# Gated cross-attention and mixture of experts: spacing GpSimd's indirect transfers and reordering the seam between the two halves

## The reference

```
x   = x + tanh(g_xattn) * xattn(layernorm(x), ctx)     # x (16, 256, 128), ctx (16, 64, 128), 16 heads of 8
x   = x + tanh(g_ffn)   * moe(layernorm(x))
xattn: q, k, v = linear maps; softmax over 64 keys, masked, / sqrt(8); output map
moe:  logits = h @ router_w + router_b;  expert = argmax(logits)       # 8 experts
      u = h @ w1[expert] + b1[expert]        # 128 -> 1024, halves a and g
      y = (a * sigmoid(g)) @ w2[expert] + b2[expert]                   # 512 -> 128
```

## Time and profile before

| | |
|---|---|
| runs | 280.64, 278.85, 280.49 us, median 280.49 |
| profiled execution | 280.14 us, span of its instructions 278.0 us |
| busy: PE, DVE, ACT, POOL | 245.6, 209.0, 156.7, 158.5 us |
| granted TensorE clock, mean | 0.976 |
| first half, about | 0 to 144 us |
| expert stage, about | 146 to 268 us |

### The profile page before, as it was taken

The page is one execution under the profiler, slowest core; times in us unless marked ns, Lnnn a source line. Parts: engine busy times, 40 slices in busy tenths (PEclk is TensorE's granted clock), DMA queues, the critical chain, the costliest instruction groups (busy, mean ns, idle before and its releaser), DMA issues.

```text
span 278.0 us, 8458 instructions
## 1 busy us (share of the span) xinstructions
PE 245.6 (88%) x2411; PEld 184.2 (66%) x2411; DVE 209.0 (75%) x608; ACT 156.7 (56%) x436; POOL 158.5 (57%) x254
## 2 busy tenths in 40 slices
PE   3979999999999989989599899399979999999950
PEld 2554445555555555544248899299979999999940
DVE  6988998898989879879649489276757777776720
ACT  5487978777566566545086765256434444444410
POOL 6505426259677585384833775826863645577740
PEclk9999999999999999999989999889999999999995
DMA  6999930000111010021244401535442222100000
GB/s 177 258 298 368 348 114 4 2 1 2 41 40 41 22 60 23 19 80 41 78 103 136 119 28 44 175 90 138 119 111 66 64 84 58 47 21 22 22 5 0
DMA packets 22412, 24.13 MB, mean 87 GB/s; under 512 B 3728, under 2 KB 19539, under 8 KB 22241
## 3 DMA queue, kind: packets, MB, share of 16 engines
q1 hardware_dynamic: 18880, 17.05, 21.7%
q0 software_dynamic: 2784, 6.43, 6.5%
q10 hardware_dynamic: 704, 0.13, 0.2%
HBM read 16.23 MB, written 8.91 MB: 90 GB/s over the span
## 4 chain that ended last, share of the span: by engine, by line
PE 80%; ACT 5%; issue 5%; another core or an unknown queue 3%; DVE 2%; POOL 2%; ACTq 1%; POOLq 0%
PE ps_B L1403 12%; PE ps_A L1403 12%; PE ps_O L1238 11%; PE ps_O L1418 6%; PE ps_B L1204 5%; PE ps_Y L1418 5%; PE ps_A L1176 4%; PE ps_Y L1249 3%; PE ps_B L1269 3%; PE ps_B L1212 3%; PE ps_B L1163 2%; PE ps_A L1181 2%; PE ps_B L1221 2%; PE ps_B L1140 1%
## 5 line engine op out<-in xcount | busy, mean ns | idle before, releaser
L486 POOL DMA_INDIRECT out_dram<-sb_early,sb_k x39 | 39.3, 1008 | 32.8 <-DVE sb_early L1054 30.2
L416 POOL DMA_INDIRECT routed_rows<-sb_xr,sb_pos x32 | 33.1, 1034 | 25.1 <-DVE sb_pos L932 9.2
L1403 PE MATMUL ps_B<-sb_early 128*128 128x128 f32 x304 | 38.8, 282 | 7.4 <-ACT sb_early L697 7.3
L870 DVE TENSOR_REDUCE sb_shift<-ps_A 128x16 bf16<-128x1024 f32 x32 | 39.0, 1218 | 6.3 <-PE ps_A L1181 5.7
L1403 PEld LDWEIGHTS ps_B<-sb_early 128*128 128x128 f32 x304 | 36.8, 198 | 8.1 <-ACT sb_early L697 8.1
L1403 PE MATMUL ps_A<-sb_early 128*128 128x128 f32 x320 | 39.1, 275 | 0.4 <-ACT sb_early L697 0.4
L621 ACT ACTIVATE sb_pT<-ps_B 128x512 f32<-128x512 f32 x64 | 33.0, 603 | 10.0 <-PE ps_B L1221 10.0
L1403 PEld LDWEIGHTS ps_A<-sb_early 128*128 128x128 f32 x320 | 37.3, 192 | 0.7 <-ACT sb_early L697 0.7
L1043 DVE SCALAR_TENSOR_TENSOR sb_qT<-ps_A,sb_b1T,sb_qT 128x128 f32<-128x128 f32 x80 | 22.5, 344 | 19.9 <-ACT sb_qT L704 12.6
L704 ACT ACTIVATE sb_qT<-ps_A,sb_b1T 128x128 f32<-128x128 f32 x80 | 22.8, 367 | 24.9 <-PE ps_A L1403 22.5
L704 ACT ACTIVATE sb_qT<-ps_B,sb_b1T 128x128 f32<-128x128 f32 x76 | 21.8, 368 | 23.7 <-PE ps_B L1403 21.1
(11 more groups left out here) (183 smaller groups left out, 464.1 us busy)
## 6 DMA issues: line engine op xcount, KB each, us to landing
sb_k<-routed_rows SPq DMA_DIRECT2D x39, 132.0 KB, 2.0
sb_w<-in_L_ffn_w_dram SPq DMA_DIRECT2D x4, 1024.0 KB, 11.2
sb_w<-in_L_ffn_w_dram SPq DMA_DIRECT2D x4, 512.0 KB, 10.2
sb_xr<-in_x_dram SPq DMA_DIRECT2D x3, 512.0 KB, 7.0
routed_rows<-routed_rows SPq DMA_DIRECT2D x8, 132.0 KB
routed_rows<-sb_pad_rows SPq DMA_DIRECT2D x7, 132.0 KB, 5.7
out_dram<-sb_early,sb_k POOLq DMA_INDIRECT x39, 2.5
sb_ctx_sb<-in_ctx_dram SPq DMA_DIRECT2D x2, 256.0 KB, 4.0
```

The lines of the kernel that those rows point to most:

```text
L416: pool.indirect_dma_start(routed[:, :], bass.IndirectOffsetOnAxis(ap=pos[:, t:t + 1], axis=0), xr[:, t, :], None, bounds_check=ROWS - 1, o ...
L486: pool.indirect_dma_start(out_rows, bass.IndirectOffsetOnAxis(ap=fr[:, k, 2 * D:2 * D + 1].bitcast(I32), axis=0), fo[:, k, :], None, bound ...
L870: dve.tensor_reduce(shift_parts[:, t, :, 0:HG], psA[:, :].rearrange("p (g h k) -> p g h k", g=G, k=C), AX.X, ALU.max).then_inc(a_max, 1)
L1403: last = pe.matmul((up_bank, gate_bank)[c](k)[:, f * P:(f + 1) * P], w_1s[:, k, o:o + P], fxT[:, k, :], start=True, stop=True)
```

## The change

GpSimd: in the loop of the first half the reciprocal roots of the first norm, the bias add and the query cast go ahead of the last scatters of a step; in the second half each step from 1 on first waits for the finish of the tile before, and the six late scatters stand one in each of the steps 5 to 10. ScalarE gives the evacuation of the transpose of sequence 13 and of the first row transpose to VectorE. VectorE: the first table ahead of the inversion of sequence 14, one expert number loaded ahead of the first weight copy instead of three, and the last group's placing and the second table one step earlier. TensorE: in the last step of the first half three of five fillers go ahead of the output map of sequence 14; the transpose of 13 goes between the two halves of the values and its logits behind the first row transpose; the four fillers ahead of that go; the second up product goes ahead of the output map of sequence 15; the last ranks go behind down product 4.

```diff
@@ -448,18 +448,23 @@
                 for n, (b0, b_end) in enumerate(GROUPS):
                     if place_at[n] == i and n <= EARLY:
                         ready = b_end * TB
+                for k in range(2 if i == B - 2 else 1):
+                    if sent < ready and room:
+                        scatter(sent)
+                        sent += 1
+                        room -= 1
+                if i in RSTD_AT:
+                    rstd(RSTD_AT[i])
+                if has(i + 1):
+                    add_bias(i + 1)
+                if streamed(i + 3):
+                    queries(i + 3)
                 while sent < ready and room:
                     scatter(sent)
                     sent += 1
                     room -= 1
                 if i == B - 2:
                     rstd_2(i - 1)
-                if i in RSTD_AT:
-                    rstd(RSTD_AT[i])
-                if has(i + 1):
-                    add_bias(i + 1)
-                if streamed(i + 3):
-                    queries(i + 3)
                 if i == 5:
                     pool.wait_ge(w_big, W_BIG)
                     pool.wait_ge(tanh_done, 1)
@@ -500,13 +505,14 @@
                     pool.wait_ge(table_ready, 2)
                 if t + 2 < FT:
                     residual(t + 2)
+                if t > 0:
+                    pool.wait_ge(fo_ready[(t - 1) % NR], (t - 1) // NR + 1)
                 if t == 0:
                     scatter(ET + 2)
                     scatter(ET + 3)
-                elif 6 <= t < 11:
-                    for k in range(2 if t == 6 else 1):
-                        scatter(late)
-                        late += 1
+                elif 5 <= t < 11:
+                    scatter(late)
+                    late += 1
                 else:
                     store(kept)
                     kept += 1
@@ -711,10 +717,8 @@
             act.wait_ge(table1_ready, 2)
             weights(0)
             act.activation(hold[:, :], tanh_g[0:1, 0:1], ACT.Sigmoid).then_inc(sigmoid_set, 1)
-            turn2_out(B - 3)
             logits_out(B - 3)
             norm2(B - 2)
-            rows(0)
             weights(1)
             act.wait_ge(b1_ready, 1)
             gates_of(0)
@@ -1021,6 +1025,17 @@
                 dve.scalar_tensor_tensor(out=tile_row[:, T1:FT], in0=r_sum, scalar=taken[:, 0:1], in1=tile_0[:, :, 0],
                                          op0=ALU.add, op1=ALU.add).then_inc(table_ready, 1)
 
+            def turn2_out(b):
+
+                dve.wait_ge(t2_psum, b + 1)
+                need(dve, lg_psum, b - 1)
+                dve.tensor_copy(h2T[:, b % 2, :], turn2_bank(b)[:, 0:S]).then_inc(t2_evac, 1)
+
+            def rows(t):
+
+                dve.wait_ge(fx_psum, t + 1)
+                dve.tensor_copy(fxT[:, t % 2, :], psB[1][:, 0:P]).then_inc(fx_ready, 1)
+
             def expert(t):
 
                 return dve.value_load(tile_expert[0:1, t:t + 1], min_val=0, max_val=E - 1)
@@ -1054,20 +1069,24 @@
                 dve.scalar_tensor_tensor(out=fo[:, k, :], in0=(psO, psY)[t % 2][:, 0:D], scalar=tanh_g[:, 1:2],
                                          in1=fr[:, k, 0:D], op0=ALU.mult, op1=ALU.add).then_inc(fo_ready[k], 1)
 
+            first_table()
             invert(B - 2)
-            first_table()
+            dve.wait_ge(table1_ready, 2)
+            dve.wait_ge(w_big, W_BIG)
+            e_0 = expert(0)
+            weights(0, e_0)
             add_residual(B - 2)
             statistics2(B - 2)
             moments2(B - 2)
-            dve.wait_ge(table1_ready, 2)
-            dve.wait_ge(w_big, W_BIG)
-            e_0, e_1, e_2 = expert(0), expert(1), expert(2)
-            weights(0, e_0)
             choose(LAST_GROUP - 1)
+            turn2_out(B - 3)
+            rows(0)
+            e_1 = expert(1)
             weights(1, e_1)
             invert(B - 1)
             place(LAST_GROUP - 1)
             gate(0, e_0)
+            e_2 = expert(2)
             weights(2, e_2)
             e_3 = expert(3)
             for t in range(FT):
@@ -1087,15 +1106,15 @@
                     tiles_taken()
                 if t == 3:
                     choose(LAST_GROUP)
-                if t == 5:
+                if t == 4:
                     place(LAST_GROUP)
                     dve.wait_ge(region_ready, LAST_GROUP + 1)
                     dve.tensor_copy(pad_i[:, :], region0[0:1, :]).then_inc(pad_ready, 1)
+                if t == 5:
+                    tiles_left()
                 if t == 6:
-                    tiles_left()
+                    second_table()
                 if t == 7:
-                    second_table()
-                if t == 8:
                     second_rows()
                     dve.wait_ge(table_ready, 2)
 
@@ -1336,6 +1355,9 @@
             for i in range(0, B):
                 if i > 0:
                     subtract_maxima(i)
+                if i == B - 1:
+                    pe.wait_ge(a_max, TB * B)
+                    spins(3, psA)
                 if has(i - 1):
                     output(i - 1)
                 if has(i - 3) and logits_at[i - 3] == i:
@@ -1347,8 +1369,7 @@
                 if has(i - 2) and i < B - 1:
                     turn2(i - 2)
                 if i == B - 1:
-                    pe.wait_ge(a_max, TB * B)
-                    spins(5, psA)
+                    spins(2, psA)
                 if i > 0 and streamed(i + 4):
                     turn_rows(i + 4)
                 if has(i + 1):
@@ -1358,13 +1379,13 @@
                         ranks(n)
                 if has(i):
                     values(i, 1)
+                    if i == B - 1:
+                        turn2(i - 2)
                     if i == 0:
                         project(1)
                         turn_rows(NF)
                     values(i, 0).then_inc(pv_done, 1)
-                if i == B - 1:
-                    turn2(i - 2)
-                if has(i - 2) and logits_at[i - 2] == i:
+                if has(i - 2) and logits_at[i - 2] == i and i < B - 1:
                     logits(i - 2)
                 if has(i + 1):
                     scores(i + 1)
@@ -1396,7 +1417,7 @@
                 if t == 0:
                     pe.wait_ge(a_max, TB * B)
                 if t == 1:
-                    pe.wait_ge(region_ready, LAST_GROUP)
+                    pe.wait_ge(region_ready, EARLY + 1)
                 for c, done in ((1, g_psum), (0, a_psum2)):
                     for f in range(FB):
                         o = c * F + f * P
@@ -1419,16 +1440,16 @@
                                      w_2[:, bass.ds(e, 1), f:f + 1, :], start=(f == 0), stop=(f == FB - 1))
                 last.then_inc(y_psum, 1)
 
-            spins(4, psA)
             turn(0)
+            logits(B - 3)
             up(0)
             turn(1)
             ranks(LAST_GROUP - 1)
             for t in range(FT):
+                if t + 1 < FT:
+                    up(t + 1)
                 if t == 0:
                     output(B - 1)
-                if t + 1 < FT:
-                    up(t + 1)
                 if t + 2 < FT:
                     turn(t + 2)
                 if t == 0:
@@ -1439,11 +1460,11 @@
                     turn2(B - 1)
                 if t == 3:
                     logits(B - 1)
-                if t == 5:
-                    ranks(LAST_GROUP)
                 if t == T1:
                     pe.wait_ge(table_ready, 2)
                 down(t)
+                if t == 4:
+                    ranks(LAST_GROUP)
 
 
 _INS = ['x', 'ctx_1024', 'mask_1x1xSxS2_ik0', 'g_xattn', 'g_ffn', 'L0_xattn_wq', 'L0_xattn_bq', 'L0_xattn_wk',
```

## The result

The changed kernel takes 277.34 us (median of 6 runs, 276.07 to 278.38) where the kernel before takes 280.65 (6 runs, 278.85 to 281.96): ratio 0.9885, interval [0.9845, 0.9925]. That is 3.3 us faster, at the edge of what can be told from no change, and a good third of the 9.3 us forecast; the range held it, the forecast did not. The profiled execution took 277.74 us with a span of 276.0, so 2.4 us under the profiled 280.14 of before.

What follows compares the result with a forecast made beforehand. It took TensorE to bound the kernel, standing still where crowded indirect transfers were thought to make its completions reach readers late. Sum: 280.14 - 5.7 + 0.3 - 1.2 - 2.3 = 271.2 us, range 268.5 to 278.5.

Steps and rivals of the forecast that it cites:

- What bounds the kernel: Whole kernel: TensorE holds 80% of the chain of waits, so gains must come from time it stands still there.
- holds: TensorE's completions reaching their readers late, by 2.60 and up to 5.4 us, with crowded indirect transfers as the working theory.
- Part 1: Expert stage, scatters after the last routing: one a step, each behind a finish; gain 5.7 us, bounds 6.4 and 0.
- Row tile 14: Its fetch waits for all scatters, the last now paced by finish 9; loss 0.3 us, within 0 to 0.7.
- Part 2: Expert stage stores: spaced one a tile, six times a pair; gain 1.2 us, bounds gain 1.6 and loss 0.8.
- Part 3: Seam between the halves: gain 2.3 us, from 3.2 without a hold and 1.4 with the whole hold.
- Part 4: Heads 12 to 14: bias add and query cast ahead of the last scatters; nothing, bound 0.7 either way.
- A: Crowding goes and the late completions with it: the forecast 271.2 us, own range 268.5 to 273.5; chance 0.48.
- B: The pad copies make the late completions at 174 to 179: 273.7 us with half left, 276.9 with all; chance 0.25.
- C: Late completions follow the number of transfers, not their spacing: 279.0 us; chance 0.13.
- D: Half clock or the norm of sequence 15 eats the seam's gain: 273.6 us; chance 0.07.
- E: Slower: each paced scatter beside the pad copies meets late completions of its own, 284.9 us; chance 0.07.

Runs made afterwards that it cites:

- x_res: Changed kernel with the residual add of tile t+2 moved between the two stores of a step; 270.73 us, ratio 0.9635.
- x_mid: Changed kernel with the second store of a step first waiting for the first quarter of gate t+1; 276.28 us, ratio 0.9859.
- x_gap: Changed kernel with only an empty GpSimd operation between the two stores of a pair; 272.14 us, ratio 0.9611.
- x_sp: x_res with GpSimd's four scatters of head step 14 spaced by the bias add and the rstd 13 operations; 271.67 us, ratio 0.9611.
- x_best: x_sp with residual 2 between step 0's two scatters, and two scatters in step 5 with residual 7 between; 269.75 us, ratio 1.0019.
- x_tail: Changed kernel without second stores: one store a step, the seven owed standing together at the end; 278.68 us, ratio 0.9931.
- seam_only: Seam and heads part of the change alone, expert stage as in the kernel before; 278.67 us, ratio 0.9917.
- b_padlate: Kernel before with the eight pad copies held back until all scatters have landed; 291.32 us.
- x_best_out: x_best with the output product of sequence 15 ahead of up product 1, as before the change; 269.61 us, ratio 1.0012.

## Why the prediction was right and wrong

**What bounds the kernel: right, on its chip.** The holds are the better part of the 10.8 us that the first profile of the kernel before has over the one without them: 6.4 at products 9 and 10 and 1.6 at product 17, both priced exactly so from TensorE's rows, and 2.9 ahead of product 0, where the seam's hold was seen and the two in the loop were not priced. That they come from crowded indirect transfers was called a theory from coincidence; x_res against x_mid, x_gap and x_sp show it. How one engine's transfers delay what another sees is not shown. That a hold might belong to the chip, not to the kernel, was not thought of, since one trace can't show it.

**Part 1, right.** Forecast 5.7 with 6.4 as the bound; measured 6.4 (the lead goes from 1.29 to 7.70 between products 5 and 10). The reserve of 0.7 was not needed. VectorE kept up, as reckoned: products 5 to 13 are 2.79 to 2.97 apart. Its bound of 0, "the copies make the hold", was the right worry for the wrong case: the copies only lengthen a crowd's hold.

**Row tile 14, right in kind.** Forecast +0.3 within 0 to 0.7; measured 0.9 (3.71 instead of 2.78). The mechanism was the one described; the fetches of the second table start at 184.18, 3.4 us behind the last scatter's issue at 180.78, and GpSimd's residual then waits 1.89 us for the DMA. Without holds it was 0.8 in the changed kernel (3.59), and x_best's earlier last scatter takes it away.

**Part 2, wrong: the step that failed.** The prediction says: "A pair had no loss behind it at 194.63 (gap 0.30), one had 0.74 at 96.36. Bounds: a gain of 1.6, and a loss of 0.8 if each of the six pairs costs 0.4. I take a gain of 1.2". The gain of 1.6 was there, but each pair costs 1.04, where one of the six was reckoned, at 0.4: (7.82 - 1.58)/6, the difference between the lags of the two profiles of the changed kernel at products 32 and 14. Six pairs make 6.2; the term came out as a loss of 4.75 instead of a gain of 1.2, and those 5.95 us are nearly all of the 6.5 between forecast and profiled time. The error is in what was called a pair. A gap of 0.30 is GpSimd's idle time behind the transfer ahead, not the spacing of the two. The store at 194.63 follows one of 193.07 that took 1.26 us, so the two start 1.56 apart, and x_res shows 1.63 to be harmless. The same trace has one pair of stores that does start 1.3 apart, and it stands right ahead of the loss at 205.02, which the prediction booked to the backlog as a whole:

```profile
200.36 0.99 POOL L486 DMA_INDIRECT out_dram<-sb_early,sb_k  x1 [0.16 <-issue]
201.65 1.06 POOL L486 DMA_INDIRECT out_dram<-sb_early,sb_k  x1 [0.30 <-issue]
```

So the 1.6 was the price of one such pair, and the trace had no free pair at all. The two rows with a price, 0.74 behind 96.36 and 1.6 behind 201.65, bracket the measured 1.04: six pairs at 0.74 are 4.4 and the sum 275.2 instead of 271.2 (the gain of 1.6 less 4.4, in place of the gain of 1.2), six at 1.6 are 9.6 and the sum 280.4. The profiled 277.74 lies between. The change replaced one pair by six.

**Part 3, right at product 3, wrong behind it.** Forecast 2.3; the lead is 2.81 at product 0 and 2.20 at product 3 (the late start of the profile and the gain of the heads, 1.1 each, cancel in it by luck), which stands 10.97 behind product 0, as reckoned (11.0). At product 4 0.8 is lost behind the scatters of 153.85 and 155.26. It is not lost in x_res, x_tail, seam_only and the runs without holds, and lost again in x_gap, x_sp and b_padlate, with the same 1.4 us between those two scatters. The hold at the seam stayed, as the middle value assumed (1.42 us ahead of the shift subtraction, 3.05 before). The row copies on VectorE took 0.42 and 0.29 us (taken as 0.7 together; 0.71):

```profile
142.11 0.42 DVE L1032 COPY sb_h2T<-ps_B 128x256 f32<-128x256 f32 x1
143.37 0.29 DVE L1037 COPY sb_early<-ps_B 128x128 f32<-128x128 f32 x1 [0.83 <-PE ps_B L1408]
```

The estimate from the Trainium skill ("VectorE: DVE Perf Modes", the section on the TRN2 errata), 0.39 and 0.26, is 0.03 us under each.

**Part 4, a term put at nothing.** "Nothing; bound 0.7 either way" left out that the kernel before has two holds in its loop, one of them the 0.74 that Part 2 quotes. The change removes both, and that is worth 1.1 us.

**Rivals.** A happened for the scatters and not for the stores. B in part, as above. C came nearest in time (279.0) and is false: x_tail and x_res have the same transfers and no hold behind the late scatters or the stores. D: not in the changed kernel's profile, but in one of x_best's and in that of x_best_out. There the Trainium skill's rule ("TensorE: Matmul & The Clock Gate", Part 1: throttled is the default, activity releases it) agrees with the row of 3.76 us at 0.52. E did not happen: the paced scatters beside the copies met no hold. But its arithmetic, a hold for every paced transfer, is what the pairs did at 1.04 each.

**What the change is worth** depends on the chip. With holds 3.3 us, of 10 to 11 that were to be had (x_res and x_sp are 10.3 and 11.5 us below the kernel before on their chips, the fastest versions there); without holds nothing (ratios 1.0004 and 1.0036). In the profiles of these two kernels on one such chip the lead of 1.64 at product 0 shrinks to 1.06 at product 3 and 0.47 at product 14, and is 0.3 at product 38.

**Left open.** Why some chips hold and others don't; each group ran on one chip at one time, so chip and time can't be told apart. Holds were there on two chips (281.0, 283.2) and in the profiles of the two kernels shown first, and absent on four (269.7, 269.0, 268.5, 269.5). For 269.0 and 268.5 the profile of a kernel with crowded transfers shows it; for the other two the time of the kernel before alone says so. Whether x_best as a whole meets a hold where there are holds: it never ran on such a chip, and its first three late scatters stand 1.70 and 1.66 apart beside the pad copies, while x_res shows only one such spacing to be free. And where the limit lies: the waits in the loop stand behind 1.43 and 1.44, 1.4 in step 0 cost 0.8 in some profiles and nothing in others, 1.56 and 1.63 cost nothing.

## What to carry to other kernels

When an engine waits for something that no engine is working on, list what else starts near it; here it was GpSimd's indirect transfers 1.3 us apart, and on a chip with holds one small operation moved between two of them was worth 1 us each time. Take the distance of two transfers from start to start; the idle time between them hides how long the first one took. When a change spreads work out, look at what it bunches instead, and price each new bunch by the worst nearby row, times their number. Before two profiles are compared by their clock times, check a row that the change can't have touched: here the first one was already 1.1 us off. Before tuning a wait that no row explains, take a second profile of the same kernel on another chip: a good part of such a gain may exist on some chips only.

## What the runs showed that was not expected

- One program, 281 or 269 us by chip with the granted clock of the span hardly different (0.976 and 0.984 in the two profiles of the kernel before) and an undisturbed tile at 2.79 us on both; most of the difference is time between a matmul's end and its reader's start, and the half clock behind the longest of these.
- A crowd of indirect transfers held what TensorE had finished 1.7 us by itself and 3.4 and 5.0 with direct copies beside it; the copies alone held nothing. The Trainium skill ("SBUF — State Buffer", the section on the two separate sides) says of the ports into that memory: "A DMA cannot be slowed by a compute op, and vice versa." The matmuls ahead of the hold agree (1.95 us, as elsewhere); what comes late is the start of the reader: TensorE's end at 173.91 is read at 179.29. Whether that has to do with these ports no run shows.
